# Gate difference in PSUM, norm shifts as one-tensor operations, and another order of stores and weight loads where attention ends

## The chip, the cores and the metric

The kernel runs on one core of one Trainium2 chip. The metric is the device time of one execution in microseconds (us); of several executions the median is taken. Engines are named as in the profile: PE (TensorE), PEld (its weight load), DVE (VectorE), ACT (ScalarE), POOL (GpSimd), and SP, whose queue (SPq) issues most of the DMAs.

## The reference

A layer norm, cross attention (16 heads, 64 keys) with a residual, a second layer norm, and a feed-forward network of one shared net and one of two routed experts, for 4096 rows of 512:

```python
x = x + xattn(layernorm(x), ctx, masks, Wq, Wk, Wv, Wo, bo)
z = layernorm(x)
one_hot = one_hot(argmax(softmax(z @ gate_w.T)), 2)
masked  = z[None] * one_hot.T[:, :, None]          # rows of the other expert are zero
routed  = (relu(masked @ w1 + b1) @ w2 + b2).sum(0)
shared  = relu(z @ sw1 + sb1) @ sw2 + sb2
out = x + routed + shared
```

Matrices are split into a high and a low float16 part, and each product is three float16 matmuls (high·high, high·low, low·high).

## The kernel before

The program has three stages, each a block; between two blocks all engines wait for one another.

**Attention** (some 110 to 530 us of the span) works on 32 tiles of 128 rows, as a software pipeline written out by hand: `body(g)` on each engine runs four values of u, and `step(engine, g, u, d, fn)` calls `fn` for tile N·g+u+d. Per tile, PE transposes the probabilities (`t_p`, L455), computes the scores of the tile two ahead (`sim`, L445), then the output (`attend`, L466). ACT runs in this order: `hi_p` (L519, high part of the transposed probabilities), `exp` (L552), two scalings of weight rows (L546, L548), `normal2` (L533, L534: second norm of the tile before, which needs shift2), `normal` (L525, L526: first norm of the tile four ahead). DVE: `residual` (L732) and its statistics, `lo_p` (L676, the low part, which `attend` waits for), masks and statistics, `sums`, `masked` (L748) and the row maximum (L753), then `shifts` (L703, L704), `shifts2` (L710, L711), `gate` (L756: (x1 − mean) times the difference of the two gate rows, summed), `pick` (L763). POOL: powers for the deviations (L615, L620), `norm` (L630), `sub` (L625), and three subtractions for low parts (L647, L643, L634). The two operations L711 and L756 read two SBUF tensors each. SP issues the loads and stores of each tile in a fixed order, in which `store_z` (L401) is last.

While attention runs, the shared net's weights are split (`load_w`, `store_w`) and stored in DRAM; the room of the attention weights in SBUF is free again after the last `sim`. Then `load_next()` transposes the first two tiles of z and loads the first quarter of the shared weights, and `load_w1_w2(q)` loads quarters 1 to 3 (L1057, L1060), all on SP, inside the attention block.

**The shared net** (545 to 1228 us) has 16 tiles of 256 rows. For each of 16 hidden chunks j, PE runs `first` (L992, 12 matmuls) and `second` of chunk j−2 (L1004, 6 matmuls); ACT runs two `relu`s (L1015, L1017) and DVE `lo_h` (L1023). Beside them the experts' weights are treated, two slices per tile (h = 0, 1), at the chunks that `AT` lists. In tiles 0 to 7 (before `PASS`) DVE runs `idle_expert` (L1351) at j = AT[h] and `largest` (L1355) at the next two chunks. From tile 8 on ACT runs `split_hi` (L1240) and DVE `split_lo` (L1342) at j = AT[h] and AT[h]+2, and SP stores the result (`store_e`, L1143, L1144); `split_hi` of a slice waits until the stores of the slice before have landed. SP's loads and stores are in one loop over the tiles; in tile 14 it also issues 8 MB of expert weights.

**The experts** (1236 to 1948 us) do the same on 17 tiles (the last of 128 rows) that are sorted by expert. The change doesn't touch this stage.

Of the kernel before, what the change touches and what calls it, by code (L numbers as in the profile page):

```python
# [10 lines left out]
ALU = mybir.AluOpType  # L11
# [4 lines left out]
P = 128  # L16
BATCH, SEQ, DM = 4, 1024, 512
# [8 lines left out]
SUB = ROWS // P  # L26
# [11 lines left out]
LN_SCALE = 2.0 ** 11  # L38
# [67 lines left out]
def xattn_ffn(nc, x, ctxT, tgt, src, wq, wkT, wvT, woT, bo, gate_w, w1, b1, w2, b2, sw1, sb1, sw2, sb2, out):  # L106
# [21 lines left out]
    with ExitStack() as ctx:  # L128
# [65 lines left out]
        with ExitStack() as at:  # L194
# [12 lines left out]
            with ExitStack() as a:  # L207
# [85 lines left out]
                pS = [banks_a, ps("pS1", [P, HK], a)]  # L293
                pk = [pS[n // 2][:, (n % 2) * 512:(n % 2 + 1) * 512] for n in range(4)]
                pP = ps("pP", [P, HK], a)
                pO = ps("pO", [P, DM], a)

                def f_dst(n, m, v):
# [37 lines left out]
                with nc.Block() as block:  # L336
                    @block.sync
                    def _(sp):
# [64 lines left out]
                        def body(g):  # L403
                            for u in range(N):
                                step(sp, g, u, 3, turn_x)
                                if not isinstance(g, int) or N * g + u + 6 >= N:
                                    step(sp, g, u, 6, load_x)
                                step(sp, g, u, 4, load_m)
                                if first_tile(g, u, 3):
                                    sp.wait_ge(f_done, NF)  # L410
                                step(sp, g, u, 1, load_r)
                                step(sp, g, u, -2, store_x1)
                                step(sp, g, u, 3, load_w)
                                step(sp, g, u, 1, store_w)
                                if last_tile(g, u):
                                    load_next()
                                step(sp, g, u, -2, store_z)
                                if isinstance(g, int) and g == SUB // N and u < 3:
                                    load_w1_w2(u + 1)
                        def load_next():  # L420

                            for u in range(2):
# [250 lines left out]
                    def _(dve):  # L673
# [26 lines left out]
                        def shifts(e, g, u):  # L700
                            e.wait_ge(S["rs_x"], count(g, u))
                            at_least(e, S["xn"], count(g, u) - 2)
                            e.tensor_scalar(rs1[:, u % 2, :], rs[:, u % 2, :], LN_SCALE, None, ALU.mult)  # L703
                            e.scalar_tensor_tensor(out=shift1[:, u % 2, :], in0=mv[:, u % 2, 0:1], scalar=-LN_SCALE, in1=rs[:, u % 2, :],  # L704
                                                   op0=ALU.mult, op1=ALU.mult).then_inc(S["rs"], 1)

                        def shifts2(e, g, u):
                            e.wait_ge(S["rs_z"], count(g, u))
                            at_least(e, S["zh"], count(g, u) - 2)
                            e.tensor_scalar(rs2[:, u % 2, :], rsz[:, u % 2, :], LN_SCALE, None, ALU.mult)  # L710
                            e.scalar_tensor_tensor(out=shift2[:, u % 2, :], in0=mv2[:, u % 2, 0:1], scalar=-LN_SCALE, in1=rsz[:, u % 2, :],  # L711
                                                   op0=ALU.mult, op1=ALU.mult).then_inc(S["rs2"], 1)

                        def stats2_done(e, g, u):
                            e.wait_ge(S["stats2"], count(g, u))
# [37 lines left out]
                            e.tensor_reduce(mx[:, u % 2, :], s[:, u % 2, :, :], AX.X, ALU.max).then_inc(S["mx"], 1)  # L753

                        def gate(e, g, u):
                            e.scalar_tensor_tensor(out=junk[:, :], in0=x1[:, u % 2, :], scalar=mv2[:, u % 2, 0:1], in1=gw[:, 1, :],  # L756
                                                   op0=ALU.subtract, op1=ALU.mult, accum_out=gg[:, u % 2, :]).then_inc(S["gd"], 1)

                        def pick(e, g, u):
# [98 lines left out]

                        dve.wait_ge(S["const_in"], 32)
                        dve.tensor_scalar(srcf[:, :], srcb[:, :], 0.0, None, ALU.is_equal).then_inc(S["src_neg"], 1)  # L860
                        dve.tensor_tensor(gw[:, 1, :], gw[:, 1, :], gw[:, 0, :], ALU.subtract).then_inc(S["src_neg"], 1)
                        dve.wait_ge(S["src_neg"], 2)

                        def body(g):
# [198 lines left out]
def shared_net(nc, room, x1_d, z_d, res_d, split_s, split_e, units, w1, w2, sb2, net_scales, consts, cols):  # L1063
# [8 lines left out]
    with ExitStack() as f:  # L1072
# [24 lines left out]
        pV = pI[:, 1, 0:SLOT_SUBS]  # L1097
        EXP_STEPS = 18
        PASS = TILES // 2
        AT = (5, 12)  # L1100

        def first_tile(g, u, d):
            return isinstance(g, int) and N * g + u + d == 0
# [11 lines left out]
        with nc.Block() as block:  # L1115
            @block.sync
            def _(sp):
                def load_z(t):
                    net.transpose(sp, t, z_d[t * TOK:(t + 1) * TOK, :])

                def load_r(t):
                    at_least(sp, S["o"], t - 1)
                    sp.dma_start(net.rb[:, t % N, :, :], net.rows(x1_d, t)).then_inc(S["r_in", t % N], 16)

                def store(t):
                    sp.wait_ge(S["ob"], t + 1)
                    sp.dma_start(net.rows(res_d, t), net.ob[:, t % N, :, :]).then_inc(S["out", t % N], 16)

                def load_e(q):

                    if 2 <= q < TILES + 2:
                        sp.wait_ge(S["seen"], 2 * (q - 1))
                        sp.wait_ge(S["cacc"], 2 * (q - 1) + 1)
                    if q >= TILES + 2:
                        sp.wait_ge(S["el"], 2 * (q - TILES - 1))
                    for i, w in enumerate((w1, w2)):
                        sp.dma_start(er[:, q % 2, i, :, :], net.rows(units(w), q % TILES)).then_inc(S[f"e_in{q % 2}"], 16)

                def store_e(q):
                    n = q - TILES  # L1140
                    sp.wait_ge(S["el"], 2 * n + 2)
                    for i, d in enumerate((e1_d, e2_d)):
                        sp.dma_start(net.rows(units(d[0]), n), eh[:, i, :, :]).then_inc(S["e_out"], 16)  # L1143
                        sp.dma_start(net.rows(units(d[1]), n), el[:, i, :, :]).then_inc(S["e_out"], 16)  # L1144

                load_e(0)
                sp.dma_start(brow[:, :], sb2.partition_broadcast(P)).then_inc(S["brow_in"], 16)
                for u in range(2):
                    sp.wait_ge(stored["x1_out", u], 16 * SUB // 2)
                    sp.wait_ge(stored["z_out", u], 16 * SUB // 2)  # L1150
                load_r(0)
                for t in range(TILES):
                    if t > PASS:
                        store_e(2 * t - 1)
                    load_e(2 * t + 1)
                    if t == TILES - 2:
                        sp.wait_ge(S["e_out"], 64 * TILES // 2)
                        load_set(nc, sp, wB, e1_d, e2_d, 0, w_in)
                    if t + 1 < TILES:
                        load_r(t + 1)  # L1160
                    if t > 0:
                        store(t - 1)
                    if t >= PASS:
                        store_e(2 * t)
                    if t + 1 < TILES:
                        load_e(2 * t + 2)
                    if t + 2 < TILES:
                        load_z(t + 2)
                store_e(2 * TILES - 1)
                store(TILES - 1)  # L1170
                enet.transpose_rows(sp, 0)
# [450 lines left out]
```

## Time and profile before

| what | value |
|---|---|
| median of 3 runs | 1953.7 us (1953.43 to 1954.43) |
| the profiled execution's own time | 1949.51 us |
| its span, first to last instruction | 1947.8 us |
| PE busy | 1843.4 us, 95% |
| DVE, ACT, POOL busy | 888.6, 820.7, 475.2 us |
| mean granted PE clock | 0.983 |

The span is the part of the execution between the first and the last instruction; the own time has a few us around it. The profiled execution is one of its own, not one of the three. A busy share is an average over three stages with different limits, so the stages are read apart below.

### The profile page before, as it was taken

The page shows a single profiled execution, that of the slowest core. Times are in us where ns is not written, and L with a number is a line of the kernel's source. Part 1 is how long each engine was busy: PE and PEld are TensorE (multiplying, and loading weights), DVE is VectorE, ACT ScalarE, POOL GpSimd, SP SyncE. Part 2 cuts the span into 40 slices and gives each one's busy share as a digit, 9 for nine tenths or more (in the row PEclk, how much of TensorE's full clock was granted, in tenths as well). Part 3 has the DMA queues.
Part 4 walks back from the last instruction along what each step waited for, and adds up shares of the span by engine and source line. Part 5 has one row for each costly group of instructions (what it writes and reads, how often), then busy time and mean ns, then how long its engine had stood idle before and what let it go on. Part 6 is the DMA issues. An engine that isn't in the chain of part 4 may idle for free. (4 is left out here: it accounts for less than half of the span.)

```text
span 1947.8 us, 33594 instructions
## 1 busy us (share of the span) xinstructions
PE 1843.4 (95%) x11584; PEld 1156.5 (59%) x11585; DVE 888.6 (46%) x1733; ACT 820.7 (42%) x1441; POOL 475.2 (24%) x443
## 2 busy tenths in 40 slices
PE   6979999999789999999999999899999999999997
PEld 5334444444356666666666666566666666666664
DVE  5968999999625334434333333322222222222222
ACT  3644554444433333334544544333333333333333
POOL 1036666666500001000001000211222111212211
PEclk9989999999989999999999999999999999999998
DMA  9235554554652322223444474721222111121200
GB/s 322 74 72 140 147 146 147 154 153 143 210 185 76 98 86 98 79 94 97 129 161 130 129 253 158 268 57 44 56 54 57 46 43 40 54 54 49 59 23 15
DMA packets 220647, 214.38 MB, mean 110 GB/s; under 512 B 121360, under 2 KB 162832, under 8 KB 220176
## 3 DMA queue, kind: packets, MB, share of 16 engines
q1 hardware_dynamic: 212640, 188.05, 32.3%
q0 software_dynamic: 7920, 25.17, 4.1%
q8 instruction: 54, 0.88, 0.2%
q14 instruction: 33, 0.27, 0.0%
HBM read 129.56 MB, written 58.98 MB: 97 GB/s over the span
## 5 line engine op out<-in xcount | busy, mean ns | idle before, releaser
L992 PE MATMUL pH<-room_a,room_w 128*128 128x256 f16 (+1 forms) x6336 | 767.7, 272 | 18.2 <-PEq L336 15.9
L1004 PE MATMUL pY<-room_w,room_a 128*128 128x512 f16 (+1 forms) x3120 | 755.2, 380 | 4.6 <-DVE room_a L1023 4.6
L992 PEld LDWEIGHTS pH<-room_a,room_w 128*128 (+1 forms) x6336 | 613.0, 98 | 197.5 <-issue 27.2
L1023 DVE TENSOR_TENSOR room_a<-room_a 128x256 f16<-128x256 f32 (+1 forms) x528 | 233.6, 443 | 910.4 <-ACT room_a L1017 908.2
L1004 PEld LDWEIGHTS pY<-room_w,room_a 128*128 128x128 f16 x3120 | 305.2, 98 | 268.0 <-DVE room_a L1023 4.8
L1015 ACT ACTIVATE room_a<-pH,e_bsel,sc 128x256 f32<-128x256 f32 (+1 forms) x272 | 151.7, 558 | 433.4 <-PE pH L992 408.6
L1015 ACT ACTIVATE room_a<-pH,b1s,sc 128x256 f32<-128x256 f32 x256 | 144.2, 563 | 391.8 <-PE pH L992 391.8
L466 PE MATMUL pO<-room_w,room_b 128*128 (+1 forms) x768 | 174.6, 385 | 26.2 <-DVE room_b L676 26.2
L1182 POOL TENSOR_TENSOR room_a<-room_a,s_brow 128x512 f32<-128x512 f32 x32 | 42.4, 1345 | 587.5 <-DVE room_a L1031 587.5
L1017 ACT ACTIVATE room_a<-pH,e_bsel,sc 128x256 f16<-128x256 f32 (+1 forms) x272 | 149.5, 550 | 0.0
L466 PEld LDWEIGHTS pO<-room_w,room_b 128*128 128x128 f16 x768 | 75.4, 99 | 123.9 <-issue 32.7
L1017 ACT ACTIVATE room_a<-pH,b1s,sc 128x256 f16<-128x256 f32 x256 | 142.2, 555 | 0.0
L1419 POOL DMA_INDIRECT rows_room<-z_split,e_iz x33 | 33.6, 1018 | 371.5 <-DVE e_iz L1410 321.4
L533 ACT ACTIVATE room_b<-room_b,shift,rs 128x512 f32<-128x512 f32 x32 | 26.0, 813 | 194.7 <-DVE shift L711 194.7
L445 PE MATMUL banks_a<-room_w,room_a 128*128 (+1 forms) x384 | 88.8, 389 | 5.4 <-DMA room_a<-room_a 5.4
L1466 POOL TENSOR_TENSOR room_a<-room_a,e_sel 128x512 f32<-128x512 f32 x33 | 43.8, 1345 | 175.5 <-DVE room_a L1031 175.5
L445 PE MATMUL pS<-room_w,room_a 128*128 (+1 forms) x384 | 85.5, 379 | 0.0
L445 PEld LDWEIGHTS banks_a<-room_w,room_a 128*128 128x128 f16 x384 | 38.4, 100 | 50.5 <-issue 10.6
L625 POOL TENSOR_TENSOR room_b<-room_b 128x1024 f32<-128x1024 f32 x32 | 62.1, 1942 | 9.1 <-DVE room_b L753 8.9
L445 PEld LDWEIGHTS pS<-room_w,room_a 128*128 128x128 f16 x384 | 37.6, 98 | 41.9
L630 POOL TENSOR_TENSOR room_b<-room_b 128x1024 f32<-128x1024 f32 x32 | 60.8, 1901 | 0.0
L1342 DVE SCALAR_TENSOR_TENSOR s_el<-s_er,sc,s_eh 128x1024 f16<-128x1024 f32 x32 | 41.1, 1285 | 24.3 <-ACT s_eh L1240 24.3
(183 smaller groups left out, 1425.2 us busy)
## 6 DMA issues: line engine op xcount, KB each, us to landing
s_er<-in_w SPq DMA_DIRECT2D x64, 512.0 KB, 5.1
room_w<-e_split SPq DMA_DIRECT2D x8, 2048.0 KB, 18.5
rows_room<-in_x SPq DMA_DIRECT2D x32, 256.0 KB, 3.1
room_a<-in_sw SPq DMA_DIRECT2D x32, 256.0 KB, 4.1
room_b<-in_x SPq DMA_DIRECT2D x32, 256.0 KB, 3.7
s_split<-room_a SPq DMA_DIRECT2D x64, 128.0 KB, 3.8
x_scratch<-room_b SPq DMA_DIRECT2D x32, 256.0 KB, 3.9
z_split<-room_b SPq DMA_DIRECT2D x32, 256.0 KB, 4.0
```

The lines of the kernel that those rows point to most:

```text
L445: mm = e.matmul(pS[u % 2][:, h * 512:(h + 1) * 512], xT[:, u % 2, c, :], f[:, k, bass.ds(b, 1), h * 512:(h + 1) * 512], start=(n == 0), st ...
L466: mm = e.matmul(pO[:, :], pt[:, q, :], f[:, bass.ds(b, 1), q, :], start=(n == 0), stop=(n == 3 * PAIRS - 1))
L625: e.tensor_tensor(v, v, mx[:, u % 2, :].unsqueeze(2).broadcast_to([P, HEADS, KEYS]), ALU.subtract).then_inc(S["sub"], 1)
L630: e.tensor_tensor(v, v, ri[:, u % 2, :].unsqueeze(2).broadcast_to([P, HEADS, KEYS]), ALU.mult).then_inc(S["prob"], 1)
L992: mm = q.matmul(self.pH[j % 2][:, 0:rows], w[:, k, j * P:(j + 1) * P], zt[:, u, k, 0:rows], start=(n == 0), stop=(n == 3 * KC - 1))
L1004: mm = q.matmul(self.pY[u][r][:, :], h[:, j % self.HR, r * P:(r + 1) * P], w[:, j, :], start=(j == 0 and n == 0), stop=(j == HC - 1 and n ...
L1015: q.activation(self.hf[:, j % self.HR, 0:rows], self.pH[j % 2][:, 0:rows], ACT.Relu, bias=b, scale=self.a1)
L1017: q.activation(self.hh[:, j % self.HR, 0:rows], self.pH[j % 2][:, 0:rows], ACT.Relu, bias=b, scale=self.a1).then_inc(self.S["hh"], 1)
L1023: q.tensor_tensor(self.hl[:, j % self.HR, 0:rows], self.hf[:, j % self.HR, 0:rows], self.hh[:, j % self.HR, 0:rows], ALU.subtract).then_in ...
L1182: v = q.tensor_tensor(net.ob[:, u, r, :], net.ob[:, u, r, :], brow[:, :], ALU.add)
L1342: dve.scalar_tensor_tensor(out=el[:, i, :, :], in0=er[:, n % 2, i, :, :], scalar=sc[:, (EW1, EW2)[i]:(EW1, EW2)[i] + 1], in1=eh[:, i, :, : ...
L1466: v = q.tensor_tensor(net.ob[:, u, r, :], net.ob[:, u, r, :], sel[:, u, :], ALU.add)
```

## The change

1. The difference of the two gate rows is written to a PSUM tensor pG (one bank, which was free) and not over a gate row in SBUF. `gate` reads it there.
2. `shifts` and `shifts2` compute mean · rs · (−LN_SCALE) as a `tensor_scalar` with rs as a per-lane scalar, where it was a `scalar_tensor_tensor` with rs as a second tensor.
3. `load_next()` stands one tile earlier in SP's order and behind that tile's store of z. Quarters 2 and 3 of the shared weights are issued in the shared net's block, first of all there.
4. `AT` is (8, 13) and not (5, 12).

```diff
+                pG = ps("pG", [P, DM], a)
...
                                 step(sp, g, u, 1, store_w)
-                                if last_tile(g, u):
+                                step(sp, g, u, -2, store_z)
+                                if isinstance(g, int) and N * g + u == SUB - 2:
                                     load_next()
-                                step(sp, g, u, -2, store_z)
-                                if isinstance(g, int) and g == SUB // N and u < 3:
-                                    load_w1_w2(u + 1)
+                                if isinstance(g, int) and g == SUB // N and u == 0:
+                                    load_w1_w2(1)
...
-                            e.scalar_tensor_tensor(out=shift1[:, u % 2, :], in0=mv[:, u % 2, 0:1], scalar=-LN_SCALE, in1=rs[:, u % 2, :],
-                                                   op0=ALU.mult, op1=ALU.mult).then_inc(S["rs"], 1)
+                            e.tensor_scalar(shift1[:, u % 2, :], mv[:, u % 2, 0:1], rs[:, u % 2, :], -LN_SCALE,
+                                            ALU.mult, ALU.mult).then_inc(S["rs"], 1)
...
-                            e.scalar_tensor_tensor(out=shift2[:, u % 2, :], in0=mv2[:, u % 2, 0:1], scalar=-LN_SCALE, in1=rsz[:, u % 2, :],
-                                                   op0=ALU.mult, op1=ALU.mult).then_inc(S["rs2"], 1)
+                            e.tensor_scalar(shift2[:, u % 2, :], mv2[:, u % 2, 0:1], rsz[:, u % 2, :], -LN_SCALE,
+                                            ALU.mult, ALU.mult).then_inc(S["rs2"], 1)
...
-                            e.scalar_tensor_tensor(out=junk[:, :], in0=x1[:, u % 2, :], scalar=mv2[:, u % 2, 0:1], in1=gw[:, 1, :],
+                            e.scalar_tensor_tensor(out=junk[:, :], in0=x1[:, u % 2, :], scalar=mv2[:, u % 2, 0:1], in1=pG[:, :],
...
-                        dve.tensor_tensor(gw[:, 1, :], gw[:, 1, :], gw[:, 0, :], ALU.subtract).then_inc(S["src_neg"], 1)
+                        dve.tensor_tensor(pG[:, :], gw[:, 1, :], gw[:, 0, :], ALU.subtract).then_inc(S["src_neg"], 1)
...
-        AT = (5, 12)
+        AT = (8, 13)
...
+                for q in range(2, Q):
+                    load_quarter(sp, wA, s1_d, s2_d, q, 1, S[f"w1_in{q}"])
+                    load_quarter(sp, wA, s1_d, s2_d, q, 2, S[f"w2_in{q}"])
                 load_e(0)
```

SP's queue where attention ends, before: `x_scratch<-room_b` is a store of x1, `z_split<-room_b` a store of z, `room_w<-s_split` half a weight quarter, and the branches are the end of the block.

```order
L397 DMA x_scratch<-room_b 128x512
L401 DMA z_split<-room_b 128x1024
L1057 DMA room_w<-s_split 128x4x512 x2
L1060 DMA room_w<-s_split 128x4x512 x2
L1057 DMA room_w<-s_split 128x4x512 x2
L1060 DMA room_w<-s_split 128x4x512 x2
L336 UNCONDITIONAL_BRANCH
L1116 UNCONDITIONAL_BRANCH
L1137 DMA s_er<-in_w 128x2x512 x2
```

The same place of the changed kernel, whose line numbers are a few higher:

```order
L398 DMA x_scratch<-room_b 128x512
L402 DMA z_split<-room_b 128x1024
L337 UNCONDITIONAL_BRANCH
L1117 UNCONDITIONAL_BRANCH
L1058 DMA room_w<-s_split 128x4x512 x2
L1061 DMA room_w<-s_split 128x4x512 x2
L1058 DMA room_w<-s_split 128x4x512 x2
L1061 DMA room_w<-s_split 128x4x512 x2
L1138 DMA s_er<-in_w 128x2x512 x2
```

Eight DMAs (four rows, "x2") have moved from ahead of the block's end to behind it, still ahead of the first load of expert weights (`s_er`).

ACT in a tile of the shared net's second half, before: pairs of L1015 and L1017 are the relus of one chunk, L1240 is `split_hi`. The piece ends at the second slice's first split.

```order
L1240 ACTIVATE s_eh<-s_er,sc 128x1024
L1015 ACTIVATE room_a<-pH,b1s,sc 128x256
L1017 ACTIVATE room_a<-pH,b1s,sc 128x256
L1015 ACTIVATE room_a<-pH,b1s,sc 128x256
L1017 ACTIVATE room_a<-pH,b1s,sc 128x256
L1015 ACTIVATE room_a<-pH,b1s,sc 128x256
L1017 ACTIVATE room_a<-pH,b1s,sc 128x256
L1015 ACTIVATE room_a<-pH,b1s,sc 128x256
L1017 ACTIVATE room_a<-pH,b1s,sc 128x256
L1015 ACTIVATE room_a<-pH,b1s,sc 128x256
L1017 ACTIVATE room_a<-pH,b1s,sc 128x256
L1240 ACTIVATE s_eh<-s_er,sc 128x1024
```

The same stretch of the changed kernel:

```order
L1244 ACTIVATE s_eh<-s_er,sc 128x1024
L1016 ACTIVATE room_a<-pH,b1s,sc 128x256
L1018 ACTIVATE room_a<-pH,b1s,sc 128x256
L1016 ACTIVATE room_a<-pH,b1s,sc 128x256
L1018 ACTIVATE room_a<-pH,b1s,sc 128x256
L1016 ACTIVATE room_a<-pH,b1s,sc 128x256
L1018 ACTIVATE room_a<-pH,b1s,sc 128x256
L1244 ACTIVATE s_eh<-s_er,sc 128x1024
```

Between the last split of slice 0 and the first of slice 1 there are three chunks where there were five.

## Rows read from the trace of the kernel before

**Rows 1.** Windows: busy us (instructions) of PE, PEld, DVE, ACT, POOL; PE clock; DMA
```profile
195.20:485.00 289.80, 267.40 (x1289) 126.72 (x1289) 271.61 (x462) 140.65 (x184) 196.56 (x185) 1.00 0.52 148
545.00:1215.00 670.00, 664.16 (x4592) 451.66 (x4593) 254.93 (x510) 287.63 (x534) 41.31 (x33) 0.99 0.39 124
```

**Rows 2.** Waits of PE: waiter, whom for, us in total, times, longest
```profile
PE pO L466 <- DVE room_b L676: 26.2, 26, 2.4
```

**Rows 3.** Timeline of PE: start us, us, what; starts of `t_p`
```profile
172.43 1.04 PE L455 MATMUL pP<-ident,room_b 128*128 128x128 f32 x8
183.67 1.04 PE L455 MATMUL pP<-ident,room_b 128*128 128x128 f32 x8
...
195.22 1.09 PE L455 MATMUL pP<-ident,room_b 128*128 128x128 f32 x8 [0.16 <-POOL room_b L630]
...
497.24 1.04 PE L455 MATMUL pP<-ident,room_b 128*128 128x128 f32 x8
```

**Rows 4.** Timeline of one attention tile
```profile
306.56 1.90 POOL L630 TENSOR_TENSOR room_b<-room_b 128x1024 f32<-128x1024 f32 x1
...
308.10 0.14 DVE L703 TENSOR_SCALAR rs<-rs 128x1 f32<-128x1 f32 x1
...
308.42 1.90 POOL L625 TENSOR_TENSOR room_b<-room_b 128x1024 f32<-128x1024 f32 x1
308.47 1.87 DVE L711 SCALAR_TENSOR_TENSOR shift<-mv,rsz 128x1 f32<-128x1 f32 x1
...
310.47 0.81 ACT L533 ACTIVATE room_b<-room_b,shift,rs 128x512 f32<-128x512 f32 x1 [6.46 <-DVE shift L711]
...
313.31 1.00 ACT L519 ACTIVATE room_b<-pP 128x1024 f16<-128x1024 f32 x1
...
314.34 1.22 DVE L676 SCALAR_TENSOR_TENSOR room_b<-pP,room_b 128x1024 f16<-128x1024 f32 x1 [0.51 <-ACT room_b L519]
...
315.72 5.35 PE L466 MATMUL pO<-room_w,room_b 128*128 x24 [0.93 <-DVE room_b L676]
```

**Rows 5.** Durations by line: ns min/median/max, first and last start
```profile
L756 DVE SCALAR_TENSOR_TENSOR room_a<-room_b,mv,room_a x32: 740/1723/2404, 159.0 to 532.0; 128x512 f32<-128x512 f32 x32
...
L732 DVE SCALAR_TENSOR_TENSOR room_b<-pO,sc,room_b x32: 742/751/752, 150.2 to 529.2; 128x512 f32<-128x512 f32 x32
...
L763 DVE TENSOR_SCALAR expert<-gg,rsz x32: 212/214/216, 161.5 to 532.8; 128x1 f32 x20, 128x1 f32<-128x1 f32 x12
```

**Rows 6.** Timeline, a copy on DVE beside POOL in the shared net
```profile
599.22 2.48 POOL L1182 TENSOR_TENSOR room_a<-room_a,s_brow 128x512 f32<-128x512 f32 x2 [53.22 <-DVE room_a L1031]
...
599.42 1.09 DVE L1277 COPY s_work<-s_work 128x32 f32<-128x32 f32 x1
```

**Rows 7.** A store of z, the landings of such stores (200 to 480 us), the next `residual`
```profile
319.51 0.43 SPq L401 DMA_DIRECT2D z_split<-room_b  x1
...
325.05 0.75 DVE L732 SCALAR_TENSOR_TENSOR room_b<-pO,sc,room_b 128x512 f32<-128x512 f32 x1
...
DMA to landing us min/median/max: 3.7/4.2/4.9
```

**Rows 8.** Timeline between attention and the shared net, and first use of expert weights
```profile
534.88 0.35 SPq L401 DMA_DIRECT2D z_split<-room_b  x1
...
541.32 3.21 SPq L1060 DMA_DIRECT2D room_w<-s_split  x2
...
545.13 6.45 PE L992 MATMUL pH<-room_a,room_w 128*128 128x256 f16 x36 [15.93 <-PEq L336]
...
560.83 1.53 DVE L1351 SCALAR_TENSOR_TENSOR cacc<-s_er,s_rb,cacc 128x512 f32<-128x512 f32 x2
```

**Rows 9.** Expert stores: tile 13, their landings (900 to 1140 us), tile 14
```profile
1122.23 0.51 SPq L1144 DMA_DIRECT2D e_split<-s_el  x1
...
DMA to landing us min/median/max: 2.5/3.3/3.8
...
1178.30 1.15 ACT L1240 ACTIVATE s_eh<-s_er,sc 128x1024 f16<-128x1024 f32 x1 [4.48 <-DMA e_split<-s_el]
...
1180.41 1.48 PE L992 MATMUL pH<-room_a,room_w 128*128 128x256 f16 x12 [1.15 <-ACT room_a L1017]
```

## The prediction, made before the changed kernel was timed

> **What bounds the kernel now.** First I read the windows by stage. In the shared net PE is busy 664.16 of 670 us [rows 1]: it is the bound there and hardly waits. In attention's steady part it is busy 267.40 of 289.80 us at a granted clock of 1.00, and DVE 271.61 [rows 1]; neither is full, so a circle of waits must set the pace. The list of PE's waits names its visible end: PE waits for DVE's L676 26 times, 26.2 us in all [rows 2]. The timeline gives the pace: `t_p` starts are 11.24 us apart while the pipeline still has slack (172.43 to 183.67), and over the 24 tiles from 195.22 to 497.24 us they are 302.02/24 = 12.58 us apart [rows 3]. Each tile thus loses 1.34 us to something that isn't PE.
>
> The timeline of one tile shows what [rows 4]. DVE's L711, the one-element shift2, takes 1.87 us. It starts at 308.47, just after POOL's L625 (308.42), and ends at 310.34, just after L625 ends (310.32). ACT had waited 6.46 us for it, then does its four norm operations (310.47 to 313.31) and only then `hi_p`, L519; DVE's L676 follows it at 314.34, and PE's L466 follows that, 0.93 us late. L676 is followed on DVE by the work that feeds POOL's next L630 and L625, and the circle is closed. `gate`, L756, has a median of 1.723 us and a minimum of 0.740 [rows 5]: it too waits for a POOL operation, but stands behind shift2 and not in the circle. What both have in common is two tensors read from SBUF. L732 has the same form and size with one of its two in PSUM, and takes 0.742 to 0.752 us in all 32 instances [rows 5].
>
> **The change part by part.**
>
> *Shifts.* The new form reads one SBUF tensor and a per-lane scalar. L763 is that very form, at 0.212 to 0.216 us in 32 instances [rows 5]; L703, a tensor_scalar without the lane scalar, took 0.14 us at 308.10, in the middle of POOL's L630 (306.56 to 308.46) [rows 4]. So I take 0.21 us for each shift. Shift2 then ends near 308.7 where it ended at 310.34, and ACT's L533 starts some 1.7 us sooner. `hi_p` and L676 come 1.7 us sooner, against the 0.93 us by which PE waits. The circle takes 12.6 − 1.7 = 10.9 us, less than the 11.24 that PE needs: PE becomes the bound of attention.
>
> *Gate.* With pG in PSUM it should take L732's 0.75 us, which is 1.0 us less of DVE's time per tile. That is off the circle and I count nothing for it, but it gives DVE slack for what follows. Writing the difference to PSUM happens once, below 1 us, in the prologue.
>
> *What is late next.* `residual` (L732) waits for a store of z two tiles back. Now that store is issued at 319.51 and lands 4.2 us later (3.7 to 4.9), at 323.7, and the residual at 325.05 has 1.3 us to spare [rows 7]. The store stands last in SP's order, which starts when POOL has made the low part of x (L634), which needs ACT's norm. ACT comes 1.7 us sooner, but POOL must first finish L625, L647 and L643, which no longer overlap with a blocked DVE; I give POOL back 0.7 us of the 1.7. The circle through the store spans two tiles. It takes 25.2 − 1.3 (spare) − 1.0 = 22.9 us at most and some 22.3 if POOL isn't late, 11.15 to 11.45 per tile. So 11.24 is the floor of the pace and 11.48 its upper end with slower landings; I take 11.35. The 24 tiles take 272.4 us: 29.6 us less (32.3 at 11.24, 26.5 at 11.48).
>
> *End of attention.* The last store of z is issued at 534.88 and takes 0.35 us. Then SP issues quarters 2 and 3 until 541.32 + 3.21 = 544.53, and PE starts at 545.13 after 15.93 us without work [rows 8]. All engines wait there for SP. With those eight DMAs behind the block's end, SP reaches it at 535.23. PE starts 0.6 us after that, as it did: 9.3 us sooner. The first quarter is issued at the same time relative to its stores as before. Quarter 2 is now issued from 535.8 and PE needs it only after eight chunks, some 20 us later, so nothing is late. The first expert weights are issued at the old clock time while PE is 9.3 us ahead. They were used at 560.83 [rows 8], chunk 5; chunk 5 would now come at 551.5, close to a landing, but AT moves that use by three chunks to 559.3, at 2.6 us a chunk (670 us over 16 tiles of 16, [rows 1]). That edit covers the other. `load_next` one tile earlier holds one store of x1 back behind its own issues; the residual that needs it stands two tiles on, behind the last attend. Bounds: 8.5 us (something else in the barrier) to 11.4 (if the first 36 matmuls, 6.45 us now [rows 8], run after the shorter pause at the rate of twelve in 1.47 us [rows 9], 4.4 us); taken 9.3.
>
> *AT in the second half.* A slice's stores must have landed when the next slice's `split_hi` starts. The tightest distance was five chunks and becomes three, 7.8 us from the `split_hi` of chunk 10. From there to the issue of the last store takes 4.0 us (split_hi 1.15 [rows 9]; split_lo 1.25, from L676 of the same 128x1024 [rows 4]; three issues of 0.51 ahead of the last, as at 1122.23 [rows 9]), and landing 3.3 (2.5 to 3.8) [rows 9]. That is 7.3 of 7.8 us: no wait in an ordinary tile. In tile 14, where the stores queue behind 8 MB of expert weights, ACT waits 4.48 us now, of which PE feels 1.15 [rows 9]; the slice comes one chunk (2.6 us) later now, and its stores 2.8 us later too. I take 0.9 us gained (−1 to 1.3).
>
> *Sum.* 29.6 + 9.3 + 0.9 = 39.8 us. From the profiled execution's own 1949.5 us that gives 1909.7. The three timed runs have a median 4.2 us above that execution, an offset that I carry over: 1953.7 − 39.8 = 1913.9, forecast 1914.
>
> **A rule that would speak against it.** A float32 copy on DVE, L1277, 128x32, took 1.09 us while POOL's L1182 ran [rows 6], though it reads one tensor; it waited like L711. The Trainium skill ("VectorE: DVE Perf Modes", section "Mode 2×_2P — use both read ports for one tensor") says that tensor_scalar and copy in float32 can read one SBUF tensor through both ports, and its page "SBUF — State Buffer" (section "SBUF: two separate sides") that the second pair is shared with GpSimd and locked for a whole instruction. By that the new shift could wait as before. L703's 0.14 us beside L630 [rows 4] speaks against it for one element per lane; the rule itself asks for an even number to halve.
>
> **The rivals.**
>
> *The new shift waits too.* Then ACT still starts at POOL's end, the pace stays at 12.58, and only the block's end and tile 14 gain: 39.8 − 29.6 = 10.2 us, 1943.5. For it: L1277. Against it: L703 and L763, 64 instances without one long one. 6%.
>
> *The store of z takes the place of shift2.* If landings grow past the spare 0.3 us, because the same bytes move in less time, each further us of landing costs half a us per tile. At 0.9 us more (landing 5.1, just above the largest now) the pace is 11.8 and 24 tiles gain 18.7 us: 28.9 in all, 1925. For it: the spare is small. Against it: DMA engines are busy 0.52 of the time [rows 1]. 20%, for 1919 to 1938.
>
> *Slower: the stores of expert slices land late.* With three chunks between, every us beyond the spare 0.5 us is a wait of ACT. Tile 14 shows that PE feels 1.15 of 4.48 us, so 3.3 are absorbed: PE loses from a landing of 3.3 + 0.5 + 3.3 = 7.1 us on. To outweigh 39.8 us over eight tiles takes 5 us each, landings of 12 us in every tile; at 13 us it is 8 · 5.9 = 47 us, 1961. None outside tile 14's neighbourhood passed 3.8 [rows 9]. 3%.
>
> *More than forecast*, below 1908: pace 11.24, a warm start after the pause. 8%.
>
> **How the numbers follow.** My own case, 1908 to 1919, has 62%; the slow store 20%, the shift that waits 6%, slower 3%, more gain 8%, and 1% for a change that is no change at all. The range 1906 to 1930 takes my case, most of the last and two thirds of the slow store's: about 8 in 10. A measurement of this kernel can tell about 0.2%, 4 us, from no change. Faster by more than that: 0.95; within it: 0.02; slower: 0.03.
>
> **What would show it.** Right: the new shift at 0.2 us and gate at 0.75 us in all instances; PE's wait for the low part gone from the middle of attention, `t_p` starts 11.3 us apart; 6 to 7 us and not 15.93 between the last attend and the shared net; no wait of ACT for expert stores outside tile 14. Wrong: shift2 with a median near 1.9 us; a `residual` that waits for z's DMA in each tile; PE waiting in chunks 8 to 15 of the shared net's first tile for weights, or in chunks 13 to 15 of tiles 8 to 15.

## The result, and the profile after

The changed kernel takes 1910.5 us (median; 1908.72 to 1911.59), the kernel before on the same chip 1953.6: a ratio of 0.978 with a 95% interval of 0.9761 to 0.9799. One of its four timed runs, 1968.77 us at a granted clock of 0.936, was in a slow state; it counts in that median (without it 1909.4) but not in the ratio or in the values in brackets. Forecast were 1914 us and a range of 1906 to 1930. On a second chip the same kernel took 1911.65 beside 1951.31, a ratio of 0.9797 (0.9784 to 0.9811).

The two profiled executions differ by 38.0 us in their spans (1947.8 and 1909.8). The tiles of the shared net are counted from one start of DVE's L1031 (L1032 after) to the next, tile 0 from PE's first matmul:

| stretch | before, us | after, us | difference |
|---|---|---|---|
| start to `t_p` of tile 5 | 195.22 | 196.18 | +1.0 |
| `t_p` of tile 5 to `t_p` of tile 29 | 302.02 | 271.27 | −30.75 |
| from there to TensorE's start in the shared net | 47.89 | 39.65 | −8.2 |
| shared net, tile 0 | 52.53 | 51.71 | −0.8 |
| shared net, tile 1 | 48.16 | 49.41 | +1.25 |
| shared net, tile 14 | 43.37 | 42.04 | −1.3 |
| all that is left | | | +0.8 |

The windows of the changed kernel over the same two stretches as [rows 1] (us, then busy us of PE, PEld, DVE, ACT, POOL; PE's granted clock; DMA share and GB/s):

```profile
196.18:467.45 271.27, 270.96 (x1346) 133.81 (x1344) 211.78 (x475) 146.84 (x192) 203.31 (x193) 1.00 0.57 162
507.10:1177.10 670.00, 665.43 (x4601) 452.76 (x4602) 255.07 (x510) 288.17 (x534) 41.16 (x33) 0.99 0.40 128
```

In attention PE is now busy for 270.96 of 271.27 us: it has become the bound, but for the 0.07 us a tile that e7 below takes off. DVE fell from 271.61 us in 289.8 to 211.78 in 271.27. The `t_p` starts, which answer to [rows 3], are 11.23 to 11.67 us apart, 11.30 in the mean:

```profile
184.94 1.04 PE L456 MATMUL pP<-ident,room_b 128*128 128x128 f32 x8
196.18 1.04 PE L456 MATMUL pP<-ident,room_b 128*128 128x128 f32 x8
...
467.45 1.04 PE L456 MATMUL pP<-ident,room_b 128*128 128x128 f32 x8
```

One attention tile, in order of time, answers to [rows 4] (lines up to L1138 stand one further down than before, later ones four):

```profile
295.54 1.90 POOL L631 TENSOR_TENSOR room_b<-room_b 128x1024 f32<-128x1024 f32 x1
...
297.33 0.20 DVE L712 TENSOR_SCALAR shift<-mv,rsz 128x1 f32<-128x1 f32 x1
297.40 1.91 POOL L626 TENSOR_TENSOR room_b<-room_b 128x1024 f32<-128x1024 f32 x1
297.45 0.74 DVE L757 SCALAR_TENSOR_TENSOR room_a<-room_b,mv,pG 128x512 f32<-128x512 f32 x1
...
297.66 0.81 ACT L534 ACTIVATE room_b<-room_b,shift,rs 128x512 f32<-128x512 f32 x1 [4.87 <-DVE shift L712]
...
300.58 0.75 DVE L733 SCALAR_TENSOR_TENSOR room_b<-pO,sc,room_b 128x512 f32<-128x512 f32 x1 [2.03 <-DMA z_split<-room_b]
...
301.98 1.21 DVE L677 SCALAR_TENSOR_TENSOR room_b<-pP,room_b 128x1024 f16<-128x1024 f32 x1
...
303.90 1.46 PE L467 MATMUL pO<-room_w,room_b 128*128 x6
```

Shift2 takes 0.20 us, though POOL adds throughout it (L631 until 297.44, L626 from 297.40); the gate runs through beside that add in 0.74; ACT starts 0.26 us after POOL's start where it had waited for POOL's end; and L467 carries no wait any more. New is `residual`, L733, which waits 2.03 us for the store of z. Over all instances (ns, minimum/median/maximum), beside [rows 5]:

```profile
L712 DVE TENSOR_SCALAR shift<-mv,rsz x32: 202/204/207, 160.3 to 503.1; 128x1 f32<-128x1 f32 x32
```
```profile
L757 DVE SCALAR_TENSOR_TENSOR room_a<-room_b,mv,pG x32: 735/737/741, 160.4 to 503.3; 128x512 f32<-128x512 f32 x32
```

And the waits of PE and of DVE (us in total, times, longest), where [rows 2] had 26.2 us in 26 waits:

```profile
PE pH L993 <- PEq L337: 7.7, 1, 7.7
...
PE pO L467 <- DVE room_b L677: 4.8, 2, 2.4
```
```profile
DVE room_b L733 <- DMA z_split<-room_b: 64.0, 28, 6.0
```

A wait of 64 us has appeared on DVE and PE hardly feels it: in the tile shown L677, the last work of DVE that PE needs, still ends 0.71 us before L467 starts. This is what the list of one engine's waits looks like when that engine is no longer on the path.

### The profile page after: what moved, and what is told of

The parts are those of the page before. It is cut to its first block and busy times, and to the rows that moved or that the text cites. A ratio compares the mean times of both kernels' runs of the same rounds, so it can differ in the third digit from the quotient of the medians.

```text
span 1909.8 us, 33594 instructions
## 1 busy us (share of the span) xinstructions
PE 1837.1 (96%) x11584; PEld 1159.2 (61%) x11585; DVE 811.1 (42%) x1733; ACT 822.2 (43%) x1441; POOL 471.2 (25%) x443
## 5 line engine op out<-in xcount | busy, mean ns | idle before, releaser
L467 PE MATMUL pO<-room_w,room_b 128*128 (+1 forms) x768 | 174.4, 384 | 4.8 <-DVE room_b L677 4.8
L467 PEld LDWEIGHTS pO<-room_w,room_b 128*128 128x128 f16 x768 | 75.8, 99 | 98.4 <-issue 6.1
L626 POOL TENSOR_TENSOR room_b<-room_b 128x1024 f32<-128x1024 f32 x32 | 61.1, 1908 | 9.2 <-DVE room_b L754 9.0
L446 PEld LDWEIGHTS pS<-room_w,room_a 128*128 128x128 f16 x384 | 37.5, 98 | 42.0
L631 POOL TENSOR_TENSOR room_b<-room_b 128x1024 f32<-128x1024 f32 x32 | 60.9, 1904 | 0.0
L733 DVE SCALAR_TENSOR_TENSOR room_b<-pO,sc,room_b 128x512 f32<-128x512 f32 x32 | 24.0, 751 | 72.7 <-DMA z_split<-room_b 64.0
```

Source lines behind the costliest of these rows:

```text
L446: mm = e.matmul(pS[u % 2][:, h * 512:(h + 1) * 512], xT[:, u % 2, c, :], f[:, k, bass.ds(b, 1), h * 512:(h + 1) * 512], start=(n == 0), st ...
L467: mm = e.matmul(pO[:, :], pt[:, q, :], f[:, bass.ds(b, 1), q, :], start=(n == 0), stop=(n == 3 * PAIRS - 1))
L626: e.tensor_tensor(v, v, mx[:, u % 2, :].unsqueeze(2).broadcast_to([P, HEADS, KEYS]), ALU.subtract).then_inc(S["sub"], 1)
L631: e.tensor_tensor(v, v, ri[:, u % 2, :].unsqueeze(2).broadcast_to([P, HEADS, KEYS]), ALU.mult).then_inc(S["prob"], 1)
```

## The experiments

Each kernel ran beside the kernel before, in three groups, each on one chip. The pace is read from the starts of `t_p` of tiles 5 and 29; "exit" is the time from the latter to PE's first matmul of the shared net. Both come from one profile of each kernel, the median from all its timed runs.

| kernel | median, us | ratio to before (95%) | pace | exit |
|---|---|---|---|---|
| before | 1953.6, 1951.8, 1951.2, 1951.3 | | 12.58 | 47.9 |
| changed | 1910.5 | 0.978 (0.9761 to 0.9799) | 11.30 | 39.65 |
| e1 shifts back | 1941.65 | 0.995 (0.9934 to 0.9967) | 12.57 | 38.3 |
| e2 gate back | 1919.0 | 0.9832 (0.9816 to 0.9849) | 11.55 | 41.3 |
| e3 shifts two wide | 1944.3 | 0.996 (0.9946 to 0.9974) | 12.59 | 39.2 |
| e6 shifts alone | 1927.1 | 0.9877 (0.9861 to 0.9894) | 11.50 | 47.6 |
| e4 order back | 1918.65 | 0.9835 (0.982 to 0.985) | 11.23 | 47.1 |
| e5 places back | 1912.7 | 0.9802 (0.9789 to 0.9816) | 11.24 | 39.0 |
| e7 no wait for z | 1909.4 | 0.9787 (0.9773 to 0.98) | 11.23 | 37.9 |
| e8 load_next later | 1909.7 | 0.9787 (0.9774 to 0.9801) | 11.28 | 37.0 |
| a1 changed, again | 1911.65 | 0.9797 (0.9784 to 0.9811) | 11.32 | 38.65 |
| v1 slots spread | 1901.5 | 0.975 (0.9736 to 0.9763) | 11.24 | 38.4 |
| v2 all three | 1898.7 | 0.9737 (0.9724 to 0.9751) | 11.23 | 37.5 |
| e9 gate back, no wait for z | 1909.1 | 0.9788 (0.9775 to 0.9801) | 11.23 | 38.3 |

**e1: the shifts back.**

```diff
-  e.tensor_scalar(shift2[:, u % 2, :], mv2[:, u % 2, 0:1], rsz[:, u % 2, :], -LN_SCALE,
-                  ALU.mult, ALU.mult)
+  e.scalar_tensor_tensor(out=shift2[:, u % 2, :], in0=mv2[:, u % 2, 0:1], scalar=-LN_SCALE,
+                         in1=rsz[:, u % 2, :], op0=ALU.mult, op1=ALU.mult)
   (shift1 likewise)
```

> The changed kernel with both norm shifts written as scalar_tensor_tensor again; gate, orders and the transfer's place stay changed. Theory (the shifts' wait beside POOL's adds carried the gain): each of the two takes 1.9 to 2.0 us again when POOL adds beside it, TensorE waits for pO in the attend of each tile again, the pace goes from 11.30 back to about 12.58 us a tile, and the time rises by 24 x 1.28 = 31 us, to about 1941. Rival (the gate's wait for POOL was what the attend waited for): the pace stays at 11.3 to 11.5 and the time within 3 us of 1910.5.

The theory holds: 1941.65 us, a pace of 12.57. One duration and one line of PE's waits say why:

```profile
L712 DVE SCALAR_TENSOR_TENSOR shift<-mv,rsz x32: 147/1874/1875, 161.2 to 533.1; 128x1 f32<-128x1 f32 x32
```
```profile
PE pO L467 <- DVE room_b L677: 25.7, 26, 2.4
```

The gate was short here (735 ns) and brought nothing by itself. A form that takes 0.147 us unhindered takes 1.87 beside POOL. One half of the expectation missed: shift1, L705, reads two SBUF tensors as well, but took 0.40 us in the median (0.47 at most), before the change too (L704, 0.40), since it starts shortly before the end of POOL's L631. So the long wait is shift2's; no run changes shift2 alone.

**e6: the shifts alone**, in the kernel before (the same edit forwards).

> The kernel before with only the two shifts made from one tensor with per-lane scalars; gate, orders and the transfer's place as before. Theory: the shifts carry nearly all of the pace, which goes from 12.58 to 11.3 to 11.6 us a tile; 24 tiles make 23 to 31 us, and 1953.6 becomes 1923 to 1930. Rival (both the shift and the gate must be early, since each alone would leave the attend behind the other's wait): the gate's 1 us a tile stays on the chain and the gain is about 24 x 0.3 = 7 us, 1946.

1927.1 us, 24.7 less than before, pace 11.50: the theory. With the old order PE's wait at the end of attention stays; and the gate, which still reads SBUF, now makes POOL's add take 2.39 us in the median, which e2 takes up:

```profile
PE pH L992 <- PEq L336: 15.8, 1, 15.8
```
```profile
L625 POOL TENSOR_TENSOR room_b<-room_b x32: 1900/2393/2467, 129.5 to 481.3; 128x1024 f32<-128x1024 f32 x32
```

**e3: two elements a lane.**

```diff
-  shift2 = sb("shift2", [P, 2, 1], F32, a)
+  shift2 = sb("shift2", [P, 2, 2], F32, a)
-  e.tensor_scalar(shift2[:, u % 2, :], mv2[:, u % 2, 0:1], rsz[:, u % 2, :], ...)
+  e.tensor_scalar(shift2[:, u % 2, :], mv2[:, u % 2, 0:2], rsz[:, u % 2, :], ...)
```

> The changed kernel with each shift made over two elements a lane instead of one (the second is the variance by the same factors and is not read). Theory (what made the shift wait was the two tensors read from SBUF): 0.2 us each as now, pace 11.3, time within 3 us of 1910.5. Rival (a tensor_scalar of one element escapes only because one element can't be read in pairs; one of two elements waits for POOL's adds as the copies do): each shift takes about 1.9 us beside POOL, the pace goes back to about 12.6 and the time to about 1941.

My theory failed and the rival held: 1944.3 us, pace 12.59. The operation still reads a single SBUF tensor, yet beside POOL's add it waits as the old form did:

```profile
L712 DVE TENSOR_SCALAR shift<-mv,rsz x32: 220/1882/1885, 161.1 to 536.1; 128x2 f32<-128x2 f32 x32
```
```profile
299.28 1.90 POOL L626 TENSOR_TENSOR room_b<-room_b 128x1024 f32<-128x1024 f32 x1
299.33 1.88 DVE L712 TENSOR_SCALAR shift<-mv,rsz 128x2 f32<-128x2 f32 x1
```

So it isn't "one tensor instead of two" that made the shift quick, but one tensor and one element. This is the rule that the prediction weighed: the Trainium skill, page "VectorE: DVE Perf Modes", section "Mode 2×_2P — use both read ports for one tensor", lets a float32 tensor_scalar from SBUF to SBUF use both ports if the outermost dimension that isn't 1 is even, or odd and equal for source and destination. The trace agrees at two elements, 1.88 us; a single element, 0.20 us, has no such dimension. No run has three elements, so that it takes an even number, and not just more than one, is not shown.

**e2: the gate back.**

```diff
-  pG = ps("pG", [P, DM], a)
-  ... in0=x1[:, u % 2, :], scalar=mv2[:, u % 2, 0:1], in1=pG[:, :],
+  ... in0=x1[:, u % 2, :], scalar=mv2[:, u % 2, 0:1], in1=gw[:, 1, :],
-  dve.tensor_tensor(pG[:, :], gw[:, 1, :], gw[:, 0, :], ALU.subtract)
+  dve.tensor_tensor(gw[:, 1, :], gw[:, 1, :], gw[:, 0, :], ALU.subtract)
```

> The changed kernel with the difference of the gate rows kept in SBUF again, so that the gate reads SBUF alone; the shifts stay tensor_scalar. Theory (the gate's wait is off the chain once the shifts are early): the gate takes 1.7 us or more beside POOL's adds, but the residual behind it waits for the store of z until about 3 us after the gate's start anyway; the pace stays at 11.3 to 11.5 and the time rises by 0 to 5 us, to 1910.5 to 1915. Rival (gate on the chain): 24 tiles by the 0.98 us that the gate waited before (1723 less 740 ns) make 24 us, 1934.

1919.0 us: 8.3 us above the changed kernel by the profiled executions (10.2 by the ratios), more than the 5 I allowed and far from the rival's 24. In the profile 5.8 us of it is pace (11.55) and 1.7 the exit. What I had not foreseen is who waits. Durations of the gate and of POOL's add:

```profile
L756 DVE SCALAR_TENSOR_TENSOR room_a<-room_b,mv,room_a x32: 739/743/2434, 161.1 to 511.5; 128x512 f32<-128x512 f32 x32
```
```profile
L625 POOL TENSOR_TENSOR room_b<-room_b x32: 1902/2392/2465, 130.6 to 484.4; 128x1024 f32<-128x1024 f32 x32
```
```profile
243.17 0.74 DVE L756 SCALAR_TENSOR_TENSOR room_a<-room_b,mv,room_a 128x512 f32<-128x512 f32 x1
243.22 2.46 POOL L625 TENSOR_TENSOR room_b<-room_b 128x1024 f32<-128x1024 f32 x1
...
247.31 0.75 DVE L732 SCALAR_TENSOR_TENSOR room_b<-pO,sc,room_b 128x512 f32<-128x512 f32 x1 [3.01 <-DMA z_split<-room_b]
...
250.11 5.35 PE L466 MATMUL pO<-room_w,room_b 128*128 x24 [0.52 <-DVE room_b L676]
...
255.39 1.90 POOL L625 TENSOR_TENSOR room_b<-room_b 128x1024 f32<-128x1024 f32 x1
255.43 2.41 DVE L756 SCALAR_TENSOR_TENSOR room_a<-room_b,mv,room_a 128x512 f32<-128x512 f32 x1
```

Whichever of the two starts first goes through and the other waits: at 243 us the gate was 0.05 us ahead and POOL's add took 2.46 us, one tile later POOL was 0.04 us ahead and the gate took 2.41. (The Trainium skill, page "SBUF — State Buffer", section "SBUF: two separate sides", says the same of an operation with two SBUF inputs: the one that starts first holds the shared ports for its whole instruction.) Since the shifts are quick, the gate mostly comes first, and POOL loses 0.5 us of every tile. That holds up POOL's L634, with it the store of z, and with that `residual`.

**e9: the gate back, and no wait for z.** The edits of e2 and e7 together; it tests the last sentence.

> The changed kernel with the gate rows' difference in SBUF again and with the residual not waiting for z's store. Theory (the gate costs nothing by its own length; beside it POOL's add is held up by 0.6 us, z's store comes later by that, and the residual waits for the store): with the wait gone the pace is 11.23 to 11.35 and the time within 2 us of the changed kernel. Rival (the gate's length or POOL's delay is on the chain by itself): the pace stays at 11.5 and the time 6 to 8 us above the changed kernel's.

POOL's add is as slow as in e2, and the time is that of the changed kernel and of e7, which differs from it only in the gate (0.9788 and 0.9787 of before), with a pace of 11.23:

```profile
L625 POOL TENSOR_TENSOR room_b<-room_b x32: 1902/2385/2474, 130.8 to 475.6; 128x1024 f32<-128x1024 f32 x32
```

So the gate's edit is worth its 8 us only through the wait for z's store. That end of the chain is shown; the links between, POOL's L634 and SyncE's order, are read from the program.

**e7: no wait for z.**

```diff
-  e.wait_ge(S["z_out", u % 2], dma_count2(g, u) - 16)
+  e.wait_ge(S["zh"], count(g, u) - 2)
```

> The changed kernel; the residual no longer waits for the landing of z's store two tiles back, only for ScalarE to have read its buffer (ScalarE's own wait for that store stays). Theory (the residual's wait of 64 us in 28 tiles lies beside other work, and TensorE is the bound): DVE's waits for z's store go, the pace goes from 11.30 to 11.24 to 11.28, the last tile gains up to 1 us: 1 to 3 us less in all. Rival (the store's landing is already what sets the pace): the pace falls below 11.2 us and the time by 5 us or more.

The pace is 11.23 us in every tile and DVE's wait for z's store is gone; the exit is 1.8 us shorter. Instead `residual` waits for PE:

```profile
DVE room_b L733 <- PE pO L467: 44.0, 31, 2.4
```

The time, 0.9787 of before, can't be told from the changed kernel's 0.978 and 0.9797; the 1 to 3 us are seen in the trace at most (24 × 0.07 + 1.8 = 3.5 us against the changed kernel, 24 × 0.01 + 1.2 = 1.4 against e5, the same attention code on the same chip), not in the clocked times. The rival, a pace below 11.2, is out.

**a1: the changed kernel again.**

> The changed kernel itself, to have it beside the three others on the same chip. The pace of attention was 11.30 us in its profile and 11.23 to 11.28 in those of three relatives whose attention code is the same or lacks one wait; theory (the landing of z's store is near the edge and differs from run to run): 11.23 to 11.35, and 0.976 to 0.980 of the kernel before. Rival (the changed kernel always loses 1.5 us there): a pace of 11.30 again.

A pace of 11.32: what the rival forecast (11.30 again), within the theory's range too. e4, e5, e8 and v1 have the same steady attention code and the same wait, and had 11.23, 11.24, 11.28 and 11.24, so the same code differs from profile to profile by up to 2 us in all. That the landing of z's store is what differs fits e7 and e9, where nothing waits for it and every tile takes 11.23 us. Two of two profiles of this very kernel had the larger value, and why is left open.

**e4: SyncE's order back.**

```diff
-  step(sp, g, u, -2, store_z)
-  if isinstance(g, int) and N * g + u == SUB - 2:
+  if last_tile(g, u):
       load_next()
-  if isinstance(g, int) and g == SUB // N and u == 0:
-      load_w1_w2(1)
+  step(sp, g, u, -2, store_z)
+  if isinstance(g, int) and g == SUB // N and u < 3:
+      load_w1_w2(u + 1)
...
-  for q in range(2, Q):
-      load_quarter(sp, wA, s1_d, s2_d, q, 1, S[f"w1_in{q}"])
-      load_quarter(sp, wA, s1_d, s2_d, q, 2, S[f"w2_in{q}"])
```

> The changed kernel with SyncE's order of before: quarters 2 and 3 of the shared net's weights are issued inside the last attention tiles, ahead of their stores, and load_next stands in the last tile. Theory (all engines wait at the end of attention's block for SyncE, which is issuing quarters): TensorE's wait ahead of the shared net goes from 7.7 back to 15.9 us and the time rises by 8 to 9 us, to about 1919. The last residual waits 1 us less for its store, which doesn't count then. Rival (the short wait came from the faster attention, not from the order): the wait stays near 8 us and the time within 2 us of the changed kernel's.

The exit is 47.1 us against 39.0 of e5 on the same chip, 8.1 more, and the time 1918.65. The last `residual` did not wait less: it started 1.9 us behind the end of the attend, for the store of z. PE's wait is back:

```profile
512.81 6.18 PE L993 MATMUL pH<-room_a,room_w 128*128 128x256 f16 x36 [16.82 <-PEq L337]
```

**e5: the slices' places back** (`AT = (8, 13)` to `AT = (5, 12)`).

> The changed kernel with the expert slices used at chunks 5 and 12 again instead of 8 and 13. Theory: tile 14 loses what it had gained, 1.3 us, and in the first tile the first slice is wanted at about 523 us, near its landing, for another 0 to 3 us: the time rises by 1 to 4 us. Rival (the place costs nothing, TensorE's lead covers it): within 1 us.

Tile 14 takes 43.70 us instead of the changed kernel's 42.04, and at chunk 5 of the first tile DVE waits for the first weights, which PE doesn't feel. In time it can't be told from the changed kernel (0.9802, beside 0.978 and 0.9797). DVE in tile 0, then ACT and PE in tile 14:

```profile
521.60 1.54 DVE L1355 SCALAR_TENSOR_TENSOR cacc<-s_er,s_rb,cacc 128x512 f32<-128x512 f32 x2 [1.75 <-DMA s_er<-in_w]
```
```profile
1137.66 1.15 ACT L1244 ACTIVATE s_eh<-s_er,sc 128x1024 f16<-128x1024 f32 x1 [4.81 <-DMA e_split<-s_el]
...
1139.78 1.48 PE L993 MATMUL pH<-room_a,room_w 128*128 128x256 f16 x12 [1.48 <-ACT room_a L1018]
```

The changed kernel's ACT waits 2.50 us there, its PE not at all:

```profile
1141.32 1.15 ACT L1244 ACTIVATE s_eh<-s_er,sc 128x1024 f16<-128x1024 f32 x1 [2.50 <-DMA e_split<-s_el]
```

**e8: load_next in the last tile, behind its store of z** (`SUB - 2` to `SUB - 1`). It answers to what the changed kernel shows at the end of attention:

```profile
484.01 3.96 SPq L975 DMA_TRANSPOSE room_a<-z_split  x2
488.01 1.30 SPq L1058 DMA_DIRECT2D room_w<-s_split  x2
...
491.92 1.68 SPq L402 DMA_DIRECT2D z_split<-room_b  x1
492.38 7.04 PE L467 MATMUL pO<-room_w,room_b 128*128 128x512 f16 x24 [2.37 <-DVE room_b L677]
...
500.47 0.75 DVE L733 SCALAR_TENSOR_TENSOR room_b<-pO,sc,room_b 128x512 f32<-128x512 f32 x1 [5.96 <-DMA z_split<-room_b]
...
506.15 0.35 SPq L402 DMA_DIRECT2D z_split<-room_b  x1
```

PE's attend ends at 499.42, but the last `residual` starts at 500.47: it waits for the store of tile 29, which SyncE issued at 491.92, behind `load_next`, and which landed 8.4 us later, twice the usual 4.1.

> The changed kernel with load_next (the first tile's transposes and the first weight quarters of the shared net) issued in the last attention tile, behind its store of z, instead of one tile earlier behind that one's. Theory (load_next holds the stores of tile 29, and the last residual waits for one of them): the residual's wait at 500 us goes and the end of attention comes 1 us sooner; the quarters land before TensorE wants them, and the time falls by 1 us. Rival (quarters 0 and 1, or the transposes, land late): the end of attention gains 1 us but TensorE waits 2 to 8 us in the first chunks of the shared net, and the time rises by 1 to 7 us.

That wait is gone (`residual` now follows attend at once, here and in v2) and the exit is 37.0 us, 1.6 to 2.6 shorter than in the changed kernel's two profiles and e5; no weight is late:

```profile
489.52 5.35 PE L467 MATMUL pO<-room_w,room_b 128*128 128x512 f16 x24 [2.37 <-DVE room_b L677]
...
494.91 0.75 DVE L733 SCALAR_TENSOR_TENSOR room_b<-pO,sc,room_b 128x512 f32<-128x512 f32 x1 [3.27 <-PE pO L467]
```

Against e5, whose exit is 2.0 us longer, 1.7 us isn't the edit's: the attend took 5.35 us at a granted clock of 1.00 where it took 7.04 at 0.76. The wait that is gone gives 2.1, but 1.8 of it is lost again: from the start of the last `residual` to PE's start 8.40 us pass here and 6.6 in e5, a1 and the changed kernel, because the last two stores now stand behind more of SyncE's weight issues (the last store of z is issued 7.1 us after the `residual` starts, 5.7 in the changed kernel). In a1, which has the order of the changed kernel, the `residual` didn't wait at all. So e8 shows the wait gone, not a gain of its own.

**v1: slots() spread.** Tile 1 of the shared net takes 6.1 us more than the others before the change and 7.4 after. DVE runs 34 small operations in one block there (the expectation says 40), 9.1 us long in the changed kernel, and PE waits for the operand behind it:

```profile
569.76 2.74 PE L1005 MATMUL pY<-room_w,room_a 128*128 128x512 f16 x6 [4.57 <-DVE room_a L1024]
```

```diff
-  def slots():
+  def slots_steps():          # the same operations, with a yield after each
       ...
+  SLOT_AT = {0: 8, 1: 8, 2: 8, 4: 5, 5: 99}
+  def slots(j):
+      for _ in range(SLOT_AT.get(j, 0)):
+          if next(slot_gen, True) is True: break
-  if j == 3 and isinstance(g, int) and g == 0 and u == 1:
-      slots()
+  if isinstance(g, int) and g == 0 and u == 1:
+      slots(j)
```

> The changed kernel with the 40 small operations of slots() spread over five chunks of the shared net's tile 1 instead of standing in one block of some 10 us at chunk 3. Theory (that block delays result and the down-projection's inputs, and TensorE waits 4.6 us and then runs at a lower granted clock): the tile takes 43 instead of 49.4 us, and the time falls by 4 to 7 us. Rival (the low clock and the wait come from elsewhere in the tile, or the spread operations delay every chunk a little): less than 2 us.

10.1 us less than the changed kernel on the same chip (1901.5 and 1911.65), and the intervals are apart. That is more than the 4 to 7 expected. Tile 1 takes 41.98 us instead of 49.58, which is 7.6 of it; attention's pace and exit were 2.3 us shorter in that profile, which the edit doesn't touch. The tile in the changed kernel, and in v1 (columns as in the windows above):

```profile
558.81:608.22 49.41, 44.84 (x294) 29.53 (x293) 24.10 (x67) 16.33 (x32) 2.50 (x2) 0.93 0.24 75
```
```profile
556.09:598.07 41.98, 41.98 (x294) 28.58 (x292) 19.61 (x43) 16.34 (x32) 2.68 (x2) 1.00 0.28 88
```

The same 294 matmuls take 44.84 us at a granted clock of 0.93 and 41.98 at 1.00: a wait of 4.57 us cost 7.4.

**v2: all three**, the edits of v1, e7 and e8.

> The changed kernel with slots() spread, load_next in the last attention tile and the residual without its wait for z's store. Theory (three separate places): the gains add up, 4 to 7 + 1 to 2 + 1 to 2 us less than the changed kernel, 1900 to 1904 on the scale of 1910.5. Rival (what the end of attention gains is lost in the first chunks of the shared net, where the quarters now land closer): no better than the spread alone.

1898.7 us, 0.9737 (0.9724 to 0.9751) of the kernel before, 13.0 us below the changed kernel on the same chip. The expectation was 1900 to 1904; what went beyond it is v1's larger gain. Against v1 it is 2.9 us less, the expected size of the other two, but the intervals overlap: the fastest version measured, though not surely faster than v1.

## Why the prediction was right

*Shifts and pace.* Forecast were 0.21 us a shift, a circle that falls below PE's need, and 11.35 us a tile; measured 0.204 and 11.30 (29.6 us forecast, 30.75 measured). e1 and e6 show the shifts' share: without them the pace gains nothing (12.57), they alone bring 24.7 us (11.50). So the forecast's term, put down to the shifts, was sized for both edits: the shifts alone gave 26 us of pace.

*Gate.* The step "that is off the circle and I count nothing for it" failed. The gate is off DVE's own circle, but beside POOL's add it takes POOL's time, and so moves the store of z. It was worth 8 to 10 us (e2), and e9 shows by which path. The sum came out right all the same, and in part by luck: the pace that I took, 11.35, rested on the circle through the store, in which I gave POOL 0.7 us back without asking what a gate in SBUF would do to POOL, and so had the gate's gain in it uncounted. As bookkeeping over the edits: 24.0 us for the shifts (1 − 0.9877 by 1953.6), 8.6 for the gate and 9.2 for the order (0.9832 and 0.9835 against 0.9788, the mean of the changed kernel's two ratios) make 41.8, against 41.4 for the whole; `AT` would add 2.7 (0.9802). Each of these ratios is known to some 3 us, and one edit put in and others taken out need not add up, so this only doesn't contradict the account.

*The store of z.* The place was right; the spare was not. The prediction had the store land 0.3 us before `residual` could start, and named "a `residual` that waits for z's DMA in each tile" as a sign of being wrong. That sign came: 28 waits, 64.0 us. It cost next to nothing because of something that the prediction didn't count, the slack behind it: L677 still ended 0.71 us before PE wanted it. The landings stayed as they were (median 4.1 us against 4.2 [rows 7]), so the rival of slower stores didn't come; e7 bounds what the wait costs at 1.7 us of pace.

*End of attention.* 9.3 us forecast, 8.2 measured (9.2 in a1), and 7.7 us of PE's wait where 6 to 7 were named. The barrier's part is right: PE started 0.6 us after SyncE's last issue, as before, and e4 gives 8.1 us for the order alone. The step that failed is "`load_next` one tile earlier holds one store of x1 back …; the residual that needs it stands two tiles on, behind the last attend". The store of z was held as well, and `residual`, which waited for that one, started 1.05 us behind the end of the attend. That wait differs by profile: 0 in a1, 2.1 in e5, and 1.9 in e4 with the old order, where `load_next` stands ahead of the same store; in e8 and v2, where it stands behind, there is none. The first 36 matmuls took 5.62 us, not 6.45, of which I had made only a bound.

*AT.* 0.9 us forecast, 1.3 measured, and 1.65 in e5. No ordinary tile waits for its stores. The wait at chunk 5 that the new place avoids exists (1.75 us, on DVE, not felt by PE).

*The new shift waits too*, at 6%, was held off by what was said against it, one element a lane: e3 is that rival made real, at 1944.3 us, where the prediction had 1943.5 for it without the other gains of pace.

*Not in the sum:* tile 1, +1.25 us, since PE's clock stayed low for longer after the same wait of 4.57 us, and +1.8 us in the start and the rest, which vary by as much among the runs.

## What to carry to other kernels

Where an operation of DVE ends, over and over, together with one of POOL, it is waiting for that, whatever its size (here one element a lane, 1.87 us): compare minimum and median of its line, look at which of the two started first, and price both, since freeing one may let it hold up the other. Before a wait that takes a removed one's place is counted as lost, follow it to the engine that bounds the stage: 64 us of waits on DVE cost at most 3.5 us here (e7), and 4.57 us on PE cost 7.4. A block of small operations in front of an operand that PE needs can be spread over the chunks; here that cost nothing that the profile shows (v1).

## What the runs showed of the hardware that I had not expected

- A float32 tensor_scalar from SBUF to SBUF takes 0.204 us beside POOL's tensor_tensor with one element a lane and 1.88 us with two (e3).
- The exclusion works in both directions, and a lead of 0.05 us decided it: POOL's 128x1024 add went from 1.90 to 2.46 us behind the gate, and the gate from 0.74 to 2.41 behind the add (e2).
- After a pause of 2.37 us, 24 matmuls took 7.04 us in one profile, at a granted clock of 0.76, and 5.35 us in another, at 1.00, with the same matmuls at the same distances and a clock of 1.00 before them (e5 and e8). In the other twelve profiles they took 6.8 to 7.0. Such a step of 1.7 us is no effect of an edit.
